# A gated recurrence over 64 head steps: a new order on three engines, and the first head's projections inside the stage ahead

## The reference

```python
xn = layernorm(x)
q, k, v = xn @ Wq, xn @ Wk, xn @ Wv              # 16 heads of 128
beta = sigmoid(xn @ Wb + bb)                     # per token and head
q = layernorm(silu(causal_dwconv(q, qconv_w, qconv_b)), qn_w, qn_b)   # 4 taps
k = layernorm(silu(causal_dwconv(k, kconv_w, kconv_b)), kn_w, kn_b)
S = (1.0 - b) * S + b * (v_t[..., :, None] * k_t[..., None, :])       # each token
o_t = einsum('bhvk,bhk->bhv', S, q_t)
s = (o * silu(xn @ Wg)) @ Wo
scores = xn @ w_r + b_r                          # top 512 tokens of each sequence
f = gelu(xn_sel @ w1 + b1) @ w2 + b2             # zero for the other tokens
out = x + s * silu(f)
```

## Time and profile before

| | us |
|---|---|
| median of 3 runs | 2729.65 (2726.43 to 2732.5) |
| the profiled execution | 2735.01, span 2733.2, mean granted TensorE clock 0.977 |
| TensorE busy | 2573.6 (94% of the span) |
| VectorE busy | 1996.9 (73%) |
| ScalarE busy | 1117.0 (41%) |
| GpSimd busy | 974.3 (36%) |
| first q projection to the start of sequence 1's | 105.64 to 578.10 |
| sequences 1 to 3, up to head 63's projection | 578.10 to 1874.60 |

### The profile page before, as it was taken

How to read it: one execution, slowest core, us unless ns; L and a number is a source line. 1 busy time by engine, 2 the same in 40 slices (tenths; PEclk the granted TensorE clock), 3 DMA queues, 4 the chain that set the end, 5 groups by cost and what they waited for, 6 DMA issues and landing times. The chain is left out here.

```text
span 2733.2 us, 44204 instructions
## 1 busy us (share of the span) xinstructions
PE 2573.6 (94%) x15744; PEld 2276.2 (83%) x15744; DVE 1996.9 (73%) x3716; ACT 1117.0 (41%) x1513; POOL 974.3 (36%) x443
## 2 busy tenths in 40 slices
PE   4689998999999999999999999999799999999997
PEld 4578888889899989988898989898688887788886
DVE  6579999999999999999999999999532211432232
ACT  5344444444444444444444444445343232422221
POOL 1135445444444444454545454544310000121211
PEclk8799999999999999999999999999899999999999
DMA  7433344453333354333335333333363010541320
GB/s 278 141 108 116 125 138 139 143 175 124 115 123 100 123 172 133 102 118 115 116 104 184 116 115 115 108 117 100 117 227 107 31 61 0 167 144 59 104 80 31
DMA packets 220860, 327.51 MB, mean 120 GB/s; under 512 B 56294, under 2 KB 156902, under 8 KB 216042
## 3 DMA queue, kind: packets, MB, share of 16 engines
q1 hardware_dynamic: 125930, 192.21, 21.4%
q10 hardware_dynamic: 86144, 109.06, 12.0%
q0 software_dynamic: 8704, 25.19, 3.0%
HBM read 237.77 MB, written 97.03 MB: 122 GB/s over the span
## 5 line engine op out<-in xcount | busy, mean ns | idle before, releaser
L939 DVE SCALAR_TENSOR_TENSOR xn_rows<-rc_ps_proj,rc_conv,xn_rows 128x1021 f32<-128x1021 f32 (+2 forms) x384 | 491.0, 1279 | 17.9 <-ACT xn_rows L841 8.8
L1106 PE MATMUL rc_ps_proj<-xt_hi,w_hi 128*128 128x512 f32 x1024 | 419.2, 409 | 27.8 <-DVE xn_rows L939 18.2
L1108 PE MATMUL rc_ps_proj<-xt_hi,w_lo 128*128 128x512 f32 x1024 | 403.9, 394 | 0.0
L1107 PE MATMUL rc_ps_proj<-xt_lo,w_hi 128*128 128x512 f32 x1024 | 402.4, 393 | 0.0
L892 ACT ACTIVATE rc_tok_k<-rc_tok_k,rc_small 128x128 f32<-128x128 f32 x512 | 204.1, 481 | 440.3 <-DVE rc_small L973 440.3
L1128 PE MATMUL rc_ps_proj<-wv_hi,xt_hi 128*128 128x256 f32 x1024 | 299.4, 292 | 26.2 <-POOL wv_lo L757 10.5
L734 POOL TENSOR_TENSOR rc_k_state<-rc_tok_k,rc_k_norm_rows 128x1024 f32<-128x1024 f32 x64 | 153.1, 2392 | 461.2 <-issue 273.1
L766 POOL TENSOR_TENSOR rc_small<-rc_small,rc_minus_half 128x16 f32<-128x16 f32 x64 | 187.0, 2923 | 361.0 <-DVE rc_small L968 361.0
L1129 PE MATMUL rc_ps_proj<-wv_lo,xt_hi 128*128 128x256 f32 x1024 | 293.9, 287 | 0.0
L1130 PE MATMUL rc_ps_proj<-wv_hi,xt_lo 128*128 128x256 f32 x1024 | 293.5, 287 | 0.0
L841 ACT ACTIVATE xn_rows<-rc_ps_proj,rc_conv 128x1024 f32<-128x1024 f32 x128 | 154.1, 1204 | 338.6 <-PE rc_ps_work L1082 317.8
(11 more groups left out here) (170 smaller groups left out, 5901.7 us busy)
## 6 DMA issues: line engine op xcount, KB each, us to landing
rc_decay_all<-scratch_decay ACTq DMA_DIRECT2D x64, 512.0 KB, 3.6
rc_cum_all<-scratch_cum ACTq DMA_DIRECT2D x64, 512.0 KB, 3.6
scratch_o<-rc_o_sb ACTq DMA_DIRECT2D x64, 512.0 KB, 3.3
w_hi<-scratch_w_split SPq DMA_DIRECT2D x48, 512.0 KB, 4.0
w_lo<-scratch_w_split SPq DMA_DIRECT2D x48, 512.0 KB, 4.7
wv_hi<-scratch_wv_split SPq DMA_DIRECT2D x24, 512.0 KB, 3.9
wv_lo<-scratch_wv_split SPq DMA_DIRECT2D x24, 512.0 KB, 4.8
scratch_w_split<-w_hi SPq DMA_DIRECT2D x16, 512.0 KB, 2.8
```

The source lines that it names most:

```text
L939: nc.vector.scalar_tensor_tensor(out=act_cm[j][:, back:], in0=projected[:, 0:L - back], scalar=conv[par][:, j, t:t + 1], in1=act_cm[j][:, ...
L1106: nc.tensor.matmul(out, hi, xt_hi[:, k, cols], start=k == 0, stop=False)
L1107: nc.tensor.matmul(out, hi, xt_lo[:, k, cols], start=False, stop=False)
L1108: last = nc.tensor.matmul(out, lo, xt_hi[:, k, cols], start=False, stop=k == KC - 1)
```

## The change

In the token stage the recurrence's small constants are loaded early (SyncE, between the weights' load and sequence 2's stores in the order of `stage_tokens`), and the accumulators of the projections become common to both stages. After the last gates TensorE does head 0's q projection, turns beta, and does head 0's k projection; ScalarE does head 0's q tap and VectorE its q convolution. The decays are formed without mask and subtraction: one_minus is written into decay, the chunks' first columns are copied to restart and then set to 0.

In the recurrence, head 0's projections, q tap and q convolution are skipped. VectorE's ranking goes behind k_state times dmat, ahead of normalise q. GpSimd's first multiply waits for the scan (dmat_done) instead of normalise q, and its subtractions change places. ScalarE's silu of k and wv_hi go ahead of the q tap.

```diff
+                    with nc.allow_non_contiguous_dma("per-channel constants"):
+                        for par in range(2):
+                            channels = slice(par * P, (par + 1) * P)
+                            for j, n_conv in enumerate("qk"):
+                                sp.dma_start(keep["conv"][par][:, j, 0:TAPS], a[n_conv + "conv_w"][channels, :]
+                                             ).then_inc(keep["conv_loaded"][par], 16)
...
+            act.wait_ge(keep["conv_loaded"][0], 16 * 4)
+            act.wait_ge(R["q_projected"], 1)
+            nc.scalar.activation(q_cm, ps_t[:, 0], ACT.Identity, bias=conv[:, 0, TAPS:TAPS + 1],
+                                 scale=conv[:, 0, PAD:TAPS]).then_inc(R["q_tap"], 1)
...
-                nc.vector.tensor_scalar(one_minus[:], beta[:], -1.0, 1.0, ALU.mult, ALU.add
-                                        ).then_inc(S["one_minus_done"], 1)
+                after(dve, S["decay_stored"], 16 * n)
+                after(dve, S["cum_done"], n)
+                nc.vector.tensor_scalar(decay[:], beta[:], -1.0, 1.0, ALU.mult, ALU.add).then_inc(S["one_minus_done"], 1)
...
-                nc.vector.tensor_tensor(decay[:], one_minus[:], inside[:], ALU.mult).then_inc(S["decay_done"], 1)
+                nc.vector.tensor_copy(chunk_starts(restart), chunk_starts(decay)).then_inc(S["restart_done"], 1)
+                dve.wait_ge(S["restart_done"], n + 1)
+                nc.vector.memset(chunk_starts(decay), 0.0).then_inc(S["decay_done"], 1)
                 dve.wait_ge(S["decay_done"], n + 1)
-                nc.vector.tensor_tensor(restart[:], one_minus[:], decay[:], ALU.subtract).then_inc(S["restart_done"], 1)
...
+            def project(pos):
+
+                pe.wait_ge(keep["w_hi_done"], 1)
+                pe.wait_ge(keep["w_lo_done"], 1)
+                for half in range(s.HALVES):
+                    cols = slice(half * BANK, (half + 1) * BANK)
+                    out = ps_t[:, pos, cols]
+                    for k in range(KC):
+                        hi, lo = keep["w_hi"][0][:, pos, k], keep["w_lo"][0][:, pos, k]
+                        nc.tensor.matmul(out, hi, xt_hi[:, k, cols], start=k == 0, stop=False)
+                        nc.tensor.matmul(out, hi, xt_lo[:, k, cols], start=False, stop=False)
+                        last = nc.tensor.matmul(out, lo, xt_hi[:, k, cols], start=False, stop=k == KC - 1)
...
                 last.then_inc(S["gate_mm"], 1)
+                if n == B - 1:
+                    project(0)
...
                 last.then_inc(S["tok_mm"], 1)
+            project(1)
...
-                    after_step(pool, "q_normed", C_.i)
+                    after_step(pool, "dmat_done", C_.i)
...
-                if A_.live:
-                    (rank_greater, rank_ties)[par](u)
-                if A_.live:
+                if A_.live and not first_done(A_.i):
                     convolve(0)
...
+                if A_.live:
+                    (rank_greater, rank_ties)[par](u)
                 if B_.live:
                     normalise()
```

More of the change, by code:

```diff
@@ L314, in _ @@
             decays(B - 1, 0)
+            dve.wait_ge(R["q_tap"], 1)
+            for t in range(PAD):
+                back = PAD - t
+                after(dve, R["q_conv"], t)
+                nc.vector.scalar_tensor_tensor(out=q_cm[:, back:], in0=ps_t[:, 0, 0:L - back], scalar=conv[:, 0, t:t + 1],
+                                               in1=q_cm[:, back:], op0=ALU.mult, op1=ALU.add).then_inc(R["q_conv"], 1)
         @block.tensor
         def _(pe):
+            def project(pos):
[9 more added lines that the diff above has]
+                        last = nc.tensor.matmul(out, lo, xt_hi[:, k, cols], start=False, stop=k == KC - 1)
+                    if half == s.HALVES - 1:
+                        last.then_inc(R["qk"[pos] + "_projected"], 1)
+                    elif pos == 1:
+                        last.then_inc(R["k_half"], 1)
             pe.wait_ge(S["consts_set"], 6)
@@ L735, in step @@
                                             ALU.mult).then_inc(S["k_weighted"], 1)
+                if par == 0 and split and not (isinstance(u, int) and u == 0):
+                    after_step(pool, "wv_hi_done", u)
+                    after_step(pool, "v_projected", A_.i - 1)
+                    after_pair(pool, wv_stored, u - 1, CACHED)
+                    stand(pool, keep["carrier_pool"])
+                    nc.gpsimd.tensor_tensor(wv_lo[:], wv_raw[:], wv_hi[:].bitcast(F32), ALU.subtract
+                                            ).then_inc(S["wv_lo_done"], 1)
+                if D_.live:
+                    after_step(pool, "q_ready", D_.i)
+                    after_pair(pool, cum_loaded[D_.par], D_.pair)
+                    after_step(pool, "outputs_mm", D_.i - 1)
+                    nc.gpsimd.tensor_tensor(q_cum[:], q_cm[D_.par][:], cum_all[D_.par][:], ALU.mult
+                                            ).then_inc(S["q_cum_done"], 1)
                 if splits(nxt.i, split):
@@ L859, in step @@
                     silu(0)
-                if A_.live:
+                    silu(1)
+                if par == 0 and split and not (isinstance(u, int) and u == 0):
+                    after_pair(act, wv_loaded, u)
+                    after_step(act, "v_projected", A_.i - 1)
+                    after_pair(act, wv_stored, u - 1, CACHED)
+                    nc.scalar.activation(wv_hi[:], wv_raw[:], ACT.Copy).then_inc(S["wv_hi_done"], 1)
+                if A_.live and not first_done(A_.i):
                     tap(0)
@@ L866, in step @@
                     tokens(0)
-                    silu(1)
-                if par == 0 and split and not (isinstance(u, int) and u == 0):
-                    after_pair(act, wv_loaded, u)
-                    after_step(act, "v_projected", A_.i - 1)
-                    after_pair(act, wv_stored, u - 1, CACHED)
-                    nc.scalar.activation(wv_hi[:], wv_raw[:], ACT.Copy).then_inc(S["wv_hi_done"], 1)
                 if splits(nxt.i, split):
```

99 lines of the change are left out of this document (49 added, 50 removed).

## The result

The changed kernel takes 2657.6 us in the median of 4 runs (2654.5 to 2660.3), the kernel before 2731.1 in 4: the ratio is 0.973, 95% interval 0.9709 to 0.9752, some 73 us less. Forecast were 2646, a range of 2632 to 2683 and 84 us.

| stretch | before | after | change | forecast |
|---|---|---|---|---|
| start to head 1's q projection | 133.6 | 107.1 | -26.5 | -23.7 |
| heads 1 to 4 | 83.9 | 83.4 | -0.5 | -4.3 |
| heads 4 to 16 (sequence 0) | 360.6 | 332.6 | -28.0 | -29.7 |
| heads 16 to 63 (sequences 1 to 3) | 1296.5 | 1273.6 | -22.9 | -27.0 |
| head 63 to the end | 858.6 | 857.9 | -0.7 | +1 |

A forecast was written before the change was run, and what follows sets the result against it. TensorE's 26.94 us step was taken as the floor, with VectorE's lateness making it wait. Terms -23.7 - 4.3 - 29.7 - 27.0 + 1 = -83.7 took the median 2729.65 to 2646 us; range 2632 to 2683, own range 2632 to 2662.

The forecast's parts named there:

- Sequences 1 to 3: Heads 16 to 63: every step at 26.95 us plus 2.8 for x loads, 1269.5 in all; -27.0 us.
- the floor: Steady step with no hole on TensorE, heads 16 to 63: 26.94 us, or 53.9 a pair against 55.0.
- the scan's and the ranking's shortening: VectorE, steady pair: scan 3.67 to 2.29 us twice, ties and slot to 1.25 and 0.22; together 6.5 of 52.1.
- Sequence 0: Heads 4 to 16: wv_lo wait gone, even steps 28.2 us, odd 26.95; 330.9 against 360.6, -29.7 us.
- the walk: Step-by-step timing of the engines' operations from a step's first projection, used to place what would be late next.
- Heads 1 to 4: Head 2's v projection loses its 3.83 us wait, plus 0.5 of the rest; -4.3 us, bounds -1 and -6.
- The fill: Token stage and head 0: head 1 starts at 109.9 us, not 133.62; -23.7 us, bounds -14 to -25.
- fourteen small DMAs: SyncE's queue, ahead of sequence 2's stores of x: at worst they hold the token stage some 5 us.
- the end: Last heads, no projection to hide under: variance may meet GpSimd's add, ties precede the normalise; +1 us (0 to +3).
- No new wait stands for q: Rival, 15%: late normalised q or k convolution makes TensorE wait at the q turn, pairs stay at 55; 2673 us.
- ties and slot stayed short: Opposite of a 4% rival: both stay stretched by GpSimd at their new place, +105 us, 2751.
- the scatter was not held: Opposite of a 5% rival: q's normalise holds back the ranks' scatter, 6 us in sequence 0's even steps, 2652.

The follow-up runs named there:

- the orders alone: The kernel before with the new orders of VectorE's ranking, GpSimd's wait and subtractions, and ScalarE's silu and wv_hi, but its old start: 2674.3 us, ratio 0.9789.

## Why the prediction was right, step by step

*Sequences 1 to 3.* The mechanism and the floor are as forecast: every step 26.96. But the text gave one cause where there are two, either of which is enough; it added up the scan's and the ranking's shortening where the first of them fills the hole. The term is 4 us short because the sequences' ends cost 6.5 (1273.6 less 47 x 26.96), not 2.8: the steps of heads 16, 32 and 48 wait for x and took 28.1, 31.1 and 28.2. In runs that have all steps there at the floor and leave those loads alone the stretch went from 1269.7 to 1279.8, so this cost varies between executions.

*Sequence 0.* wv_lo ends 12.35 us into the even step (12.5 forecast), the add 19.35 (19.6), one variance operation is held 1.86 (2), and the step takes 27.9 (28.2). What the walk lacked is the jump back of head 8, 4 us more than the other even steps. The trace of before had the same jump, with 3.0 us between VectorE's branch and its next instruction, but when that branch came, the k_state multiply and the normalise were still queued, and they covered it. After the change the slot waits for the ties, VectorE's instruction list stops there, only the 2.2 us normalise is left when the branch comes, and the jump takes 5.3. That the new wait of GpSimd costs 6 us here, and pays nowhere beside the ranking's move, the prediction did not see: it counted the scan's 1.4 us as a gain and the later chain as its price, in different stretches, and never asked what the one would be without the other.

*Heads 1 to 4* is the term that was wrong: -0.5, not -4.3. The wait for wv_lo did go: the orders alone, with the old start, bring this stretch to 80.4, which is -3.5. But the shorter start left the load of head 2's raw weights uncovered: head 1's step takes 25.7 us, where it takes 23.7 before and with the orders alone, and 23.8 with the weights ahead of the stores. The load's arrival varies too: with four pairs written out, its place unchanged, the step took 24.1. The last 1 us is not traced. The prediction walked the stores of x on SyncE's queue, not the next weights.

*The fill*, 26.5 and not 23.7, was under-sized: the last gate matmul ends at 88.5, not 90.8.

```profile
88.15 0.39 PE L383 MATMUL tk_ps_gate<-xt_hi,tk_w_lo 128*128 128x512 f32 x1
```

The windows from 30 to 60 us, before and after, with the columns of rows 1:

```profile
30.00:60.00 30.00, 20.42 (x95) 17.21 (x94) 20.22 (x33) 21.17 (x26) 1.64 (x1) 0.75 0.77 296
...
30.00:60.00 30.00, 20.26 (x111) 17.08 (x109) 20.69 (x45) 23.13 (x27) 1.98 (x2) 0.89 0.77 295
```

The granted clock is 0.89 where it was 0.75; how much of the 2.3 us that explains was not tried. The fourteen small DMAs stand ahead of the stores of x of sequence 1, the third in the stage's order, and not of sequence 2's. SyncE issues the first of these stores at 69.21, where it did at 63.10 before; the stage still ends earlier than forecast. And some 7 us of the fill hang on the ranking's move, which the text listed under another heading.

*The sum* is 5 short of the 84 us in the profiled executions, and 10 in the medians, and the errors have both signs: the fill gave 3 us more than its term, the stretches behind it 10 less, the end 2 more. That the fill's surplus makes up for part of the rest is luck. The lower end of the forecast's own range, 2632, does not follow from the three terms named with it, which give 2635.

*The rivals.* No new wait stands for q, ties and slot stayed short, and the scatter was not held: it starts 0.9 us into the normalise in the even step above and takes 1.06 us, as it does in the mean of its 30 times, and as before. That shows more than the gather of the earlier trace rows, which began ahead of the normalise beside it. The rule of the Trainium skill that spoke for the other ("SBUF — State Buffer", "Who interferes with whom", on a tensor_scalar that takes both port pairs) does not show here.

## What to carry to other kernels

When an engine is late by one microsecond in a step, several edits may each give back that microsecond, and their gains don't add: try them one by one, and drop the ones that then only cost. When a start gets shorter, ask which loads it was covering; when the end of a loop's body gets a wait, ask what is queued behind the branch.

## What the runs showed of the hardware

The jump back in sequence 0's loop took VectorE 3.0 us before the change, hidden by queued work, and 5.3 after, with 3.8 us of idle time. The ten jumps back of the later loop took 0.2 us each and cost nothing; with more code written out ahead, 3.9 to 5.8 us, with about 2.9 us of idle time (29.2 over ten). A packet of an instruction queue began within each of the long jumps, and in none of the short ones.

A 128x16 operation of 0.17 to 0.19 us took 1.8 to 2.4 us where a GpSimd operation of 2.4 had started just ahead of it. A ties comparison that started first was not held (1.26 us), and the slot behind it was (1.88). The hold works the other way as well: a gather that GpSimd sent out 0.45 us after the start of a scan took 2.60 us before the change (at 1923.14) and after it (at 1846.03), where its neighbours took 1.0 to 1.1.
